# First cross attention of a Perceiver-like block: another order of the SP queue, and another start for head 0

## What is computed

```python
def _L0_xattn_ref(qkv, y):                  # qkv: layernorm(x), y: ctx_2048 (1, 4096, 512)
    q = qkv.reshape(bs * N_HEADS, ch, length)            # 16 heads, 16 channels, 512 queries
    k = v = y.reshape(bs * N_HEADS, ch, -1)              # 16 channels, 8192 keys
    scale = 1.0 / math.sqrt(math.sqrt(ch))
    weight = jnp.einsum('bct,bcs->bts', q * scale, k * scale)
    weight = jax.nn.softmax(weight.astype(jnp.float32), axis=-1)
    a = jnp.einsum('bts,bcs->bct', weight, v)
x = x + _L0_xattn_ref(_layernorm(x, axis=-1), ctx_2048)
```

## Time and profile before

| | us |
|---|---|
| median of 3 runs | 1379.47 |
| the profiled execution | 1378.92 |
| its span on the core | 1377.1 |
| PE busy (share of the span) | 1337.2 (97%) |
| DVE busy | 1098.5 (80%) |
| ACT busy | 970.5 (70%) |
| POOL busy | 156.2 (11%) |
| first `pre` product starts | 20.52 |
| first reduction to maxima starts | 21.36 |
| first score product starts | 49.63 |

### The profile page before, as it was taken

One profiled execution on the slowest core, in us unless ns is written; L12 is line 12 of the kernel. 1 busy time (PEld: TensorE's weight loads), 2 busy tenths in 40 slices (PEclk: granted clock), 3 DMA queues, 4 the chain that ended last, 5 costly groups with the idle time before them and its releaser, 6 DMA issues. The chain is left out here.

```text
span 1377.1 us, 28335 instructions
## 1 busy us (share of the span) xinstructions
PE 1337.2 (97%) x10623; PEld 883.4 (64%) x10623; DVE 1098.5 (80%) x2195; ACT 970.5 (70%) x1892; POOL 156.2 (11%) x216
## 2 busy tenths in 40 slices
PE   3999999999999999999999999999999999999999
PEld 3544444444444444444458999999988874668998
DVE  5899999998999999997877666666668759887665
ACT  1499999998999999999574555555544631785553
POOL 4122222122222222112000000000000000000000
PEclk9899999999999999999999999999999999999999
DMA  7665556655666555565204755555529614204651
GB/s 190 123 144 126 118 140 161 154 144 131 149 159 132 130 133 130 125 92 79 100 1 151 298 186 187 185 186 188 190 91 370 244 69 177 69 1 131 181 190 39
DMA packets 75914, 199.51 MB, mean 145 GB/s; under 512 B 35576, under 2 KB 43680, under 8 KB 64128
## 3 DMA queue, kind: packets, MB, share of 16 engines
q1 hardware_dynamic: 75600, 197.69, 50.9%
q10 hardware_dynamic: 192, 0.20, 0.1%
HBM read 170.64 MB, written 23.80 MB: 141 GB/s over the span
## 5 line engine op out<-in xcount | busy, mean ns | idle before, releaser
L754 ACT ACTIVATE probs<-bank 128x512 f32<-128x512 f32 x1024 | 541.8, 620 | 51.4 <-PE bank L812 49.1
L672 DVE TENSOR_REDUCE pm<-bank 128x1 f32<-128x512 f32 x736 | 466.4, 682 | 49.3 <-PE bank L793 48.8
L812 PE MATMUL bank<-qst,kst 52*128 52x512 f32 (+1 forms) x1024 | 336.3, 437 | 6.1 <-DMA qst<-nscratch 5.8
L793 PE MATMUL bank<-kst,qst 48*128 48x512 f32 x904 | 315.2, 451 | 21.5 <-DMA qst<-qsplit 20.5
L824 PE MATMUL bank<-probs,vext 128*32 128x256 f32 (+3 forms) x4024 | 294.9, 394 | 0.7
L812 PEld LDWEIGHTS bank<-qst,kst 52*128 52x128 f32 (+1 forms) x1024 | 163.8, 187 | 195.0 <-DVE pm L672 93.8
L1602 PE MATMUL bank<-e_xhi,e_hi 128*128 128x256 f32 (+1 forms) x768 | 217.4, 283 | 0.3 <-DVE e_xlo L283 0.2
L1602 PE MATMUL bank<-e_xhi,e_lo 128*128 128x256 f32 (+1 forms) x768 | 217.3, 283 | 0.0
L1602 PE MATMUL bank<-e_xlo,e_hi 128*128 128x256 f32 (+1 forms) x768 | 217.2, 283 | 0.0
L824 PEld LDWEIGHTS bank<-probs,vext 128*32 128x32 f32 x4024 | 92.3, 109 | 117.2 <-issue 103.4
L793 PEld LDWEIGHTS bank<-kst,qst 48*128 48x128 f32 x904 | 140.6, 189 | 31.2 <-DMA qst<-qsplit 20.5
(11 more groups left out here) (251 smaller groups left out, 1764.9 us busy)
## 6 DMA issues: line engine op xcount, KB each, us to landing
raw<-wall SPq DMA_DIRECT2D x43, 1536.0 KB, 6.5
kst<-kscratch SPq DMA_DIRECT2D x192, 128.0 KB, 4.5
kscratch<-ksplit SPq DMA_DIRECT2D x15, 1024.0 KB, 4.4
kraw<-ctx_rows SPq DMA_DIRECT2D x16, 512.0 KB, 6.0
vraw<-ctx_vt SPq DMA_DIRECT2D x16, 512.0 KB, 6.1
ctxT<-ctxT SPq DMA_DIRECT2D x8, 1024.0 KB, 9.7
nat<-ctx_chunks SPq DMA_DIRECT2D x6, 1024.0 KB, 19.0
weights<-wscratch SPq DMA_DIRECT2D x16, 256.0 KB, 5.6
```

The costliest lines, as they stand in the source:

```text
L672: nc.vector.tensor_reduce(max_at(p, 1), bank[:, pre_bank(p), :], AX.X, ALU.max).then_inc(pre_reduced, 1)
L754: nc.scalar.activation(probs[:, (XST * k + n) % PR, :], bank[:, score_bank(XST * k + n), :], ACT.Exp, scale=XSCALE).then_inc(probs_ready, 1)
L793: ins = nc.tensor.matmul(bank[:, pre_bank(p), :], qst[64 * j:64 * j + KR, h, tt * P:tt * P + P], keys, start=True, stop=True)
L812: nc.tensor.matmul(bank[:, score_bank(s), :], kst[64 * j:64 * j + rows, h % 2, m * P:m * P + P], qst[64 * j:64 * j + rows, h, :], start=Tr ...
```

## The change

On the SP queue, `load_stack(h+1, 0)` moves behind `stack_negmax(2h)` in every head. At the start of head 0:

- `X` is loaded tile by tile, tile 1 only when tile 0 has landed.
- Head 0's first key half is loaded straight from the input into stacked form (`first_raw`): 8 DMAs of 16 partitions by 8 KB, four on SP ahead of `load_raw(0)`, four on ScalarE's queue ahead of everything. VectorE makes the stack from it in two instructions over 128 x 2048: the raw number times a mask that is one on the low rows (rounded to the high part there, zero elsewhere), and the raw number minus that. `pre` product 0 waits for this (`FIRST_KEYS`), as do the marks.
- The other halves keep the way over `kscratch`. Head 0's two parts go in one store (`store_split(0)`), and `load_stack(0, 1)` follows when that has landed.
- VectorE norms tile 0 with the helpers of the later stages and splits it; then the two key instructions; then mean, variance and scale of tile 1. GpSimd norms and splits tile 1 (`second_queries`) behind its other early work.
- The six query DMAs of head 0 are shared, three on SP and three on ScalarE's queue. ScalarE splits the high keys after its three.
- GpSimd sets the marks first.

The hunks below are, in this order: the SP queue ahead of its loop, the same in the loop, GpSimd, VectorE, ScalarE's queue, and TensorE's `pre`.

```diff
-            sp.dma_start(X[:, :, :], x.rearrange("(a p) d -> p a d", p=P)).then_inc(x_loaded, 16)
+            sp.dma_start(X[:, 0, :], x[0:P]).then_inc(x_loaded, 16)
+            for row in range(0, 64, XC):
+                sp.dma_start(first_raw[row:row + XC, :], first_keys[:, 0:XK // 2]).then_inc(first_loaded, 16)
             load_raw(0)
+            sp.wait_ge(x_loaded, 16)
+            sp.dma_start(X[:, 1, :], x[P:]).then_inc(x_loaded, 16)
             load_raw(1)
             load_pairs(1)
...
-            sp.wait_ge(stack_lo[0], 192)
+            for row, part in Q_ROWS:
+                sp.wait_ge(qsplit_ready, part + 1)
+                sp.dma_start(qst[64 + row:64 + row + XC, 0, :].bitcast(F32), qsplit[0:XC, part, 0, :].bitcast(F32)).then_inc(stack_lo[0], 16)
+            store_split(0)
+            sp.wait_ge(split_stored, 16)
             load_stack(0, 1)
-            sp.wait_ge(qsplit_ready, 4)
...
                 if h == 0:
                     load_v(0)
                     sp.wait_ge(const_set, 2)
+                    sp.wait_ge(dve_step.sem, FIRST_KEYS)
...
-                if h < XH - 1:
-                    load_stack(h + 1, 0)
...
                 stack_negmax(NS * h)
                 if h < XH - 1:
+                    load_stack(h + 1, 0)
                     load_apart(h + 1, 0)
...
+            def second_queries():
+                pool.wait_ge(dve_step.sem, SECOND_SCALED)
+                nc.gpsimd.tensor_scalar(xn[:, 1, :], X[:, 1, :], g.mv[:, 1, 0:1], g.rstd[:, 1, :],
+                                        ALU.subtract, ALU.mult).then_inc(g.xn_ready, 1)
...
             dve.wait_ge(x_loaded, 16)
-            norm_dve(g, dve, link)
...
+            tile_spread(g, 0, 0, link)
+            tile_scale(g, dve, 0, 0, link)
...
+            dve.wait_ge(first_loaded, FIRST_LOADS)
+            link(nc.vector.tensor_scalar(first_high[:, :], first_raw[:, :], low_row[:, :], None, ALU.mult))
+            link(nc.vector.tensor_tensor(kst[:, 0, 0:XK // 2], first_raw[:, :], first_high[:, :].bitcast(F32), ALU.subtract))
+            dve.wait_ge(x_loaded, 32)
+            tile_spread(g, 0, 1, link)
+            tile_small(g, dve, 0, 1, link)
...
+            for row in range(0, 64, XC):
+                nc.scalar.dma_start(first_raw[64 + row:64 + row + XC, :], first_keys[:, XK:XK + XK // 2]).then_inc(first_loaded, 16)
...
+                if p == 0:
+                    pe.wait_ge(dve_step.sem, FIRST_KEYS)
```

More of the change, by code:

```diff
@@ L40 @@
 Q_ROWS = [(0, 0), (XC, 0), (2 * XC, 1)]
+FIRST_LOADS = 8 * 16
+FIRST_KEYS = 9
+SECOND_SCALED = 15
 FIRST_BUSY = 4
@@ L96, in stacked @@
 def stacked(h, half):
-    return [192, 96][half] * (h // 2 + 1) + 48 * (h // 2 + h % 2)
+    return [192, 96][half] * (h // 2 + 1) + 48 * (h // 2 + h % 2) - 96 * (1 - half) * (1 - h % 2)
 def score_bank(s):
@@ L189, in setup @@
     return g
[L193 to L215, removed]
 def roots(k, a):
-    return TA * k + a
+    return TA * k + a + 1
 def turned_bank(k, a):
@@ L595, in _ @@
             nc.gpsimd.memset(marks[0:2, 1, :].bitcast(F32), 0.0).then_inc(const_set, 1)
+            split(0)
+            split(1)
+            split_apart(1)
             nc.gpsimd.tensor_copy(g.identb[:, :], ident[:, :]).then_inc(g.ident_ready, 1)
@@ L600, in _ @@
             pool.wait_ge(const_set, 4)
+            second_queries()
             values(0)
@@ L649, in link @@
                 dve.wait_ge(dve_step.sem, dve_step.inc(ins))
+            dve.wait_ge(g.ident_ready, 2)
+            link(nc.vector.tensor_reduce(low_row[:, :], ident[:, :].rearrange("p (j r c) -> p r j c", j=2, c=XC)[:, 1], AX.XY, ALU.add))
             dve.wait_ge(x_loaded, 16)
[L652 to L657 removed]
+            tile_spread(g, 0, 0, link)
+            tile_scale(g, dve, 0, 0, link)
+            dve.wait_ge(g.xn_ready, 1)
+            nc.vector.tensor_copy(qsplit[:, 0, 0], xn[:, 0, :]).then_inc(qsplit_ready, 1)
+            dve.wait_ge(qsplit_ready, 1)
+            nc.vector.tensor_tensor(qsplit[:, 1, 0], xn[:, 0, :], qsplit[:, 0, 0].bitcast(F32), ALU.subtract).then_inc(qsplit_ready, 1)
+            dve.wait_ge(first_loaded, FIRST_LOADS)
[4 more added lines that the diff above has]
+            tile_small(g, dve, 0, 1, link)
+            link(nc.vector.scalar_tensor_tensor(out=g.rstd[:, 1, :], in0=g.std[:, 1, :], scalar=1.5, in1=g.rstd[:, 1, :],
+                                                op0=ALU.add, op1=ALU.mult))
             def turn_negmax(k):
@@ L736, in lend @@
                 nc.scalar.activation(excess[:, i % 2, :], bank[:, pre_bank(p), :], ACT.Relu).then_inc(excess_ready, 1)
+            for row in range(0, 64, XC):
+                nc.scalar.dma_start(first_raw[64 + row:64 + row + XC, :], first_keys[:, XK:XK + XK // 2]).then_inc(first_loaded, 16)
             act.wait_ge(g.ident_ready, 2)
             nc.scalar.activation(g.warm[:, :], ident[:, 0:1], ACT.Sqrt)
+            tile_root(g, act, 0, 0)
+            for row, part in Q_ROWS:
+                act.wait_ge(qsplit_ready, part + 1)
+                nc.scalar.dma_start(qst[row:row + XC, 0, :].bitcast(F32), qsplit[0:XC, part, 0, :].bitcast(F32)).then_inc(stack_lo[0], 16)
             act.wait_ge(kraw_loaded[0], 16)
             nc.scalar.copy(ksplit[:, 0, :], kraw[:, 0, :]).then_inc(split_step, 1)
-            act.wait_ge(g.var_ready, 1)
-            nc.scalar.activation(g.std[:, :, :], g.var[:, :, :], ACT.Sqrt).then_inc(g.std_ready, 1)
-            for row, part in Q_ROWS:
-                act.wait_ge(qsplit_ready, part + 1)
-                for j in range(2):
-                    nc.scalar.dma_start(qst[64 * j + row:64 * j + row + XC, 0, :].bitcast(F32),
-                                        qsplit[0:XC, part, 0, :].bitcast(F32)).then_inc(stack_lo[0], 16)
+            tile_root(g, act, 0, 1)
             for k in range(XN):
```

37 lines of the change are left out of this document (15 added, 22 removed).

## The result

The changed kernel takes 1384.68 us (median of 8 runs) against 1379.41 (8 runs) for the one before, a difference of 5.3 us. The ratio worked out from the single runs, which is not the quotient of the medians, is 1.0049, with a 95% interval from 1.0029 to 1.0069: slower by 6.8 us, or 4.0 to 9.5. The prediction was 1372.6 with a range to 1376.5, so it was wrong, and wrong in sign. The profiled execution took 1384.56 with a span of 1382.8 (1377.1 before).

A forecast was written before the change was run, and what follows sets the result against it. Once scores flow the cross attention runs at the engines' pace; the maxima's way bounds the start. Start 3.5 plus loop 3.3 is 6.8 us off the profiled 1378.92: 1372.1, median 1372.6, range 1366.5 to 1376.5.

The forecast's parts named there:

- The loop's term: Cross attention loop: storing maxima ahead of the stacked keys removes late maxima in even stages, 3.3 us gain (1 to 4.6).
- such waits: TensorE's waits for late maxima in even stages of the loop, 3.2 us in four places, expected to go.
- rival E: Loop: stacked keys of the next head land late, so the kernel is slower, 1417 or 1385 us; chance 0.07.
- the start's term: Start of head 0: maxima stored ahead of the keys, first score at 46.15 instead of 49.63, 3.5 us gain (1 to 7).
- The norm and the first keys' way: Start: tile 0 done at 8.6, keys ready at 15.1, first reduction at 17.3 instead of 21.36, 4.1 us earlier.
- rival C: Start gives almost nothing: first keys late or the two subtractions block one another, marks 3 us further; 1375.6 us, chance 0.12.
- The clock: After the first score: the gap stays about as long, so the slow clock stays as it was, no gain.
- Reaching the end undiminished: After the cross attention: later stages are paced by their own engines, so a gain reaches the end undiminished.

The follow-up runs named there:

- e4: Changed kernel with load_stack(h, 1), the second key half, issued one stage later, behind stack_negmax(2h-1): 1374.39 us, ratio 0.9971.
- e8: Kernel before, old start, with load_stack(h+1, 0) behind stack_negmax(2h) and the second key half issued behind the odd maxima: 1372.65 us, ratio 0.9963.
- e2: Changed kernel with the old order, load_stack(h+1, 0) ahead of stack_negmax(2h), in every head, so only the new start: 1380.6 us, ratio 1.0023.
- e3: Changed kernel with the new order in head 0 alone, old order from head 1 on: 1377.06 us, ratio 0.9989.
- e9: Changed kernel with one wait, so that GpSimd's subtraction of head 0's keys begins when VectorE's key subtraction has ended: one execution, 1383.54 us.
- e16: e4 with marks DMAs cut to 128 of 4096 columns, GpSimd filling zeros, output wrong (small marks): 1373.68 us, ratio 0.9953.
- e15: The same kernel as e8, run again: 1372.62 us, ratio 0.9965.

## Why the prediction was wrong, step by step

**The loop's term, 3.3 us of gain: the step that failed.** I wrote that such waits should go, and that what the move delays is `load_stack(h+1, 0)`. The first half was right, for even stages: landings from 4.1 to 1.8, no stage over 19.2 but odd ones. But I followed only the step that was moved, and asked only whether its own consumer would be late (rival E), not which small transfer comes next on the same queue. The premise that the odd maxima "have nothing before them" was wrong: the stretch that the earlier trace rows leaves out has six stacked loads, raw keys and values, issued until 96.2. The odd landing was 1.42 only because these were through when the store came at 102.59. Six loads more, 768 KB, on that side used the slack up. Measured, the term is 6.4 of loss instead of 3.3 of gain: 9.7 of the 12.5 us by which the forecast for the profiled execution, 1372.1, missed its 1384.56; the start's term has the other 2.8. A slower rival was on my list, but with the wrong victim, and so at 0.07. That its 1385 lies at the measured time is luck: no product waited for stacked keys in the loop, and by its own terms a third of the heads gives 15 less 6.8, so 1387.6.

**The premise of its size.** I took 3.3 as the wait of 3.2 and some clock. Before's excess over 19.0 per stage is 4.8, 3.1 of it in one stage, so the size was fair. In e4 and e8 the loop gives 4.0 and 4.6 us (551.8 and 551.2 against 555.8) when neither side is loaded. Those are single executions, and the old order also ran in 552.9 and 553.0 (e2, e3), with no such stage; by medians of one group e4 is 2.7 below e3.

**The start's term, 3.5: mis-sized, 1.24 at the first score, 0.7 at stage 2.** By my steps, forecast and measured:

| | forecast | measured |
|---|---|---|
| tile 0 split | 8.6 | 9.15 |
| first keys landed | 11 | 11.77 |
| masked product / subtraction | 1.7 / 2.29 | 1.29 / 2.29 |
| keys ready | 15.1 | 15.4 |
| first reduction | 17.3 | 18.62 |
| kraw 0 landed | 12.4 | 12.76 |
| head 0's split stored | 15.8 | 17.61 |
| queries of head 1 issued | 25.4 | 26.99 |
| marks issued | 30.8 | 32.16 |
| maxima stored, landed | 37.0, 43.5 | 38.75, 45.55 |
| first score | 46.15 | 48.39 |

The norm and the first keys' way were each within 0.8. Two steps slipped. First, GpSimd's subtraction beside VectorE's: 3.63, not 2.34, and the store of the split at 17.61. That was rival C's mechanism, by the Trainium skill's page SBUF — State Buffer, section "Who interferes with whom"; the trace agrees (3.63 beside, 2.34 behind). It moved the marks, by 1.4 us and not by the 3 of that rival, and through them the maxima's landing, whose distance from the marks' issue, 13.4, is close to the forecast 12.7. Second, I had the queries in before VectorE was through with tile 1, at 17.3. The six query DMAs took 6.4 to 7.1 us to land, the last issued at 10.66, and TensorE began at 17.71. The changed kernel's trace puts that start down to an instruction of VectorE (L219), which TensorE's wait for the key subtraction, over at 15.4, doesn't include. The run with GpSimd's wait (e9) names the queries:

```profile
17.58 1.65 PE L803 MATMUL bank<-kst,qst 48*128 48x512 f32 x6 [17.58 <-DMA qst<-qsplit]
```

So neither keys (15.4) nor VectorE (18.0) set the first product but the queries, as in the earlier trace rows, and the first pair's own 0.9 came on top. I had taken their landing as given and had no row under it.

**The clock.** I forecast no gain from it at the start, which held: 10.2 us at 0.50 as before. The reasoning did not: I said it stays because the gap stays, and e16 has no such gap, and 0.50 for 13.7 us.

**Reaching the end undiminished.** From the store of stage 31 on, yes: 737.7 in both. At the start, no, in the profiled executions: 1.24 at the first score was 0.7 at stage 2, and 2.2 was 0.8 and 0.4 with small marks, where the medians have 1.7.

## What to carry to other kernels

When a transfer is moved behind a small, urgent one on a queue, write down the whole cyclic order of the queue with its bytes, and look at what stands ahead of every urgent transfer, not only the one that you meant to free: the backlog goes in front of another. Large loads with slack should be shared out over the gaps between the urgent ones, and issued right behind the one and not shortly ahead of the next. Then the move that by itself made this kernel slower (ratio 1.0067) is part of one that makes it faster (0.9963). Measure a loop by the period of one recurring small event: stages at the bare period and those above it show at once how late a transfer may be.

## What the runs showed of the hardware that I had not expected

- A late input can cost more than its wait, and by a different amount each time: landings of 6.1 to 6.2 us cost 1.6, 3.1 and 7.7 us, with waits of 1.5, 1.7 and 3.4 us and 0, 3.4 and 10.2 us of granted clock 0.50 behind them.
- The clock fell soon after the first score in a kernel (e16) in which TensorE had idled at most 0.64 us at a time (clock 0.51 from 48 to 62 us), and two executions of one kernel (e8, e15) had it at 0.50 for 6.8 and 3.4 us, 11 us apart.
- Four DMAs of four partitions by 16 KB took 5.1 to 7.1 us of SP's queue to issue and held back a store on the other queue: 12 us to land instead of 4.0.
- VectorE is held up beside GpSimd in other pairs too: in the new start with small marks VectorE's cast of 128 x 512 (L657 there), 0.43 us by itself, took 3.70 beside a fill by GpSimd:

```profile
5.85 7.24 POOL L590 MEMSET kst<- 32x4096 f32 x2
...
9.67 3.70 DVE L657 CAST qsplit<-xn 128x512 fp32r<-128x512 f32 x1
```
